# The targets of a pair on VectorE in the sparse feed-forward, and two copies in a row in the attention

## What is computed

```python
x = x + tanh(g_xattn[1]) * attention(layernorm(x), ctx)       # 16 heads of 64, 32 batches of 128 tokens
x = x + tanh(g_ffn[1]) * experts(layernorm(x))

# attention, per batch
q, k, v = inputs_q @ Wq, inputs_kv @ Wk, inputs_kv @ Wv
p = softmax(q @ k.T / 8 + rel_bias)
out = (p @ v) @ Wo

# experts: each token goes to 4 of 16 experts, and to a shared one
g, u = x @ gate_proj.T, x @ up_proj.T
y = (silu(g) * u) @ down_proj.T          # weighted, and summed over the 4 chosen
```

## Time and profile before

| | us |
|---|---|
| median of 3 runs | 1489.69 (1484.29 to 1493.74) |
| the profiled execution | 1486.57, span 1484.9 |
| attention | about 425 to 1085 us of the span |
| sparse feed-forward | about 1085 to 1485 us |

### The profile page before, as it was taken

One profiled execution on the slowest core, in us unless ns is written; L12 is line 12 of the kernel. 1 busy time (PEld: TensorE's weight loads), 2 busy tenths in 40 slices (PEclk: granted clock), 3 DMA queues, 4 the chain that ended last, 5 costly groups with the idle time before them and its releaser, 6 DMA issues. The chain is left out here.

```text
span 1484.9 us, 28060 instructions
## 1 busy us (share of the span) xinstructions
PE 1171.9 (79%) x9258; PEld 1069.9 (72%) x9258; DVE 945.7 (64%) x2039; ACT 789.5 (53%) x2201; POOL 531.4 (36%) x659
## 2 busy tenths in 40 slices
PE   3766413999489999999999998998649998778764
PEld 2555213898478888888888888897648997778664
DVE  4888594554166666656776577767757864335666
ACT  3555313555256666656665666656546675446441
POOL 4443135464200000110016510455153578788541
PEclk9676556999789999999999999999779999989896
DMA  3339772564330000010003310233176566657995
GB/s 91 114 127 259 228 132 83 144 163 132 63 98 9 9 8 1 23 30 2 8 23 125 125 30 1 75 126 123 42 249 209 162 193 192 198 167 220 293 287 208
DMA packets 139523, 177.12 MB, mean 119 GB/s; under 512 B 21984, under 2 KB 120448, under 8 KB 139392
## 3 DMA queue, kind: packets, MB, share of 16 engines
q1 hardware_dynamic: 110928, 122.62, 29.1%
q0 software_dynamic: 17792, 43.14, 9.0%
q10 hardware_dynamic: 10672, 9.65, 2.2%
HBM read 107.28 MB, written 68.09 MB: 118 GB/s over the span
## 5 line engine op out<-in xcount | busy, mean ns | idle before, releaser
L1617 ACT ACTIVATE attend_s<-attend_s,attend_less 128x128 f32<-128x128 f32 x512 | 198.4, 392 | 108.6 <-DVE attend_less L1758 108.6
L2269 POOL DMA_INDIRECT answers<-moe_yb,moe_dst x160 | 158.1, 988 | 94.2 <-ACT moe_yb L2364 56.0
L1572 POOL TENSOR_TENSOR router_xn<-rest_acc,router_mv 128x512 f32<-128x512 f32 x12 | 12.6, 1046 | 443.2 <-DVE router_rs L1234 387.1
L1635 ACT ACTIVATE attend_pt<-attend_psS 128x1024 f32<-128x1024 f32 x64 | 65.6, 1025 | 95.6 <-PE attend_psS L1909 95.4
L81 PE MATMUL moe_psU<-moe_wh,moe_xl 128*128 (+1 forms) x384 | 113.3, 295 | 0.0
L82 PE MATMUL moe_psU<-moe_wl,moe_xh 128*128 (+1 forms) x384 | 111.9, 291 | 0.0
L83 PE MATMUL moe_psU<-moe_wh,moe_xh 128*128 (+1 forms) x384 | 111.7, 291 | 0.0
L1202 POOL DMA_INDIRECT slots<-router_row,router_idx x80 | 80.6, 1007 | 79.7 <-DMA router_row<-normed_rows 61.5
L1756 DVE SCALAR_TENSOR_TENSOR attend_s<-attend_psS,held_bias 128x1024 f32<-128x1024 f32 x64 | 78.0, 1218 | 44.2 <-PE attend_psS L1902 44.1
L2422 DVE TENSOR_TENSOR moe_it<-moe_it,moe_psU 128x256 f32<-128x256 f32 x96 | 40.2, 418 | 102.8 <-ACT moe_it L2346 102.4
L81 PE MATMUL attend_psJ<-attend_xh,held_low 128*128 128x256 f32 x256 | 81.0, 316 | 26.0 <-DVE attend_q_t L1793 22.8
(11 more groups left out here) (386 smaller groups left out, 4118.5 us busy)
## 6 DMA issues: line engine op xcount, KB each, us to landing
moe_xg<-slots SPq DMA_DIRECT2D x160, 129.0 KB
moe_both<-answers SPq DMA_DIRECT2D x28, 512.0 KB, 5.1
router_row<-normed_rows SPq DMA_DIRECT2D x40, 256.0 KB, 2.9
slots<-mix_zero SPq DMA_DIRECT2D x4, 2048.0 KB, 18.4
layer_raw<-in_wi_dram SPq DMA_DIRECT2D x8, 1024.0 KB, 5.0
layer_raw<-in_wo_dram SPq DMA_DIRECT2D x8, 1024.0 KB, 7.0
moe_raw<-in_gex_dram SPq DMA_DIRECT2D x17, 384.0 KB, 4.1
moe_both<-normed_rows SPq DMA_DIRECT2D x24, 256.0 KB, 3.8
```

What stands on the lines that cost most here:

```text
L1617: last = nc.scalar.activation(s[:, g, j, :], s[:, g, j, :], ACT.Exp, bias=less[:, g, j:j + 1], accum_out=sm[:, g, j:j + 1])
L2269: nc.gpsimd.indirect_dma_start(out=R.YT[q], out_offset=bass.IndirectOffsetOnAxis(ap=dst[:, r % NM, s:s + 1], axis=0), in_=yb[:, r % NY, s, ...
```

## The change

In the attention, VectorE's second copy moves in front of normed(b, 0), so that the copies of us[0] and us[1] follow each other. In the sparse feed-forward, targets moves from GpSimd to VectorE, into turn j for pair j + 2, behind i_low(j - 1); it waits for the rows of the pair (x_in) and, from the ninth routed pair on, for the scatter of the pair 8 before (y_free). The separate wait for aside is gone, as VectorE makes that table itself. aside is laid out with the two numbers of a pair side by side.

```diff
                 evacuate(n, us[0], to(0))
+                evacuate(n, us[1], to(1))
                 normed(b, 0)
-                evacuate(n, us[1], to(1))
...
-    AHEAD = 4
...
-        aside = left[:, 2 * 3 * 64:2 * 5 * 64].bitcast(I32).rearrange("p (q s j) -> p q s j", q=2, s=2)
+        aside = left[:, 2 * 3 * 64:2 * 5 * 64].bitcast(I32).rearrange("p (q j s) -> p q j s", q=2, s=2)
...
-            for r in range(AHEAD):
-                targets(ROUTED[r])
             for r, j in enumerate(ROUTED):
-                if r + AHEAD < len(ROUTED):
-                    targets(ROUTED[r + AHEAD])
                 scatter(j)
...
+            def targets(j):
+
+                r, q = NTH[j], KIND[j]
+                dve.wait_ge(x_in[j % NX], x_count(j))
+                if r >= NM:
+                    scattered(dve, r - NM)
+                at = r - sum(TILES_OF[0:q])
+                v.tensor_tensor(dst[:, r % NM, :], xg[:, j % NX, :, D + 1].bitcast(I32), aside[:, q, at], ALU.add).then_inc(d_up, 1)
...
-                v.tensor_scalar(rows(aside[:, q]), psR[:, 3 * 64:5 * 64], lane[:], float(R.answer_rows[q]), ALU.is_gt, ALU.mult).then_inc(aside_up, 1)
+                v.tensor_scalar(aside[:, q].rearrange("p j s -> p s j"), psR[:, 3 * 64:5 * 64].rearrange("p (s j) -> p s j", s=2), lane[:], float(R.answer_rows[q]), ALU.is_gt, ALU.mult).then_inc(aside_up, 1)
...
                 if 1 <= j <= PAIRS_ALL:
                     i_low(j - 1)
+                if j + 2 < PAIRS_ALL and not is_shared(j + 2):
+                    targets(j + 2)
```

More of the change, by code:

```diff
@@ L2288, in send @@
                                              in_=row[:, h % NS, a, :], in_offset=None).then_inc(sent[h % NS], 16)
[L2290 to L2300, removed]
             nc.gpsimd.iota(steps128[:], [[P, MOST * 3]], base=0, channel_multiplier=0, **small)
```

## The result

The changed kernel took 1467.51 us (median of 4 runs, 1464.26 to 1471.58) beside 1487.12 us for the kernel before (4 runs): a ratio of 0.985 [0.982, 0.988]. Its profiled execution took 1471.58 us, with a span of 1469.9. Run again beside 17 runs of the kernel before (median 1490.88), it gave 0.9858 [0.9838, 0.9877]. So it is about 1.5% faster, clear of the noise. The chances put slightly more on "within 1%" (0.49) than on "faster" (0.46), and that was wrong.

The account below looks back on a forecast made before the run. It took TensorE, waiting for VectorE's copies, to bound the attention, and TensorE, GpSimd, SyncE, then DMA the sparse feed-forward. Attention -14.7 and feed-forward -1.8 made -16.5 us: 1486.57 to 1470, plus 3.1 for the median, 1473; range 1465 to 1484.

Parts of the forecast that it names:

- The other five have one long wait in place of two ...: nothing: Attention, five router-middle half-steps where VectorE comes late from router work (one wait 2.66 us): no gain.
- the four of the table's last row: Attention half-steps 0, 19, 29 and 30, the remaining ones: about 1 us less in all.
- 0.71 and 0.83 us a half-step: Attention without router middle: gain when TensorE's second wait goes, 0.71 us for q, 0.83 for k, counted between starts.
- rival 2: Attention: TensorE gains only its idle entries, 9 us, because something held for slack (o_low) binds; 1479 us, chance 0.14.
- ScalarE's hold on the router middles: Attention: with router rows in the middle, the output product awaits ScalarE's last copy, leaving 0.26 of 0.71 us.
- Half-steps with the router's inverse, near 0.9: Attention: three k half-steps with the router's inverse between the copies would gain near 0.9 us each.
- rival 3: Attention: fewer stops let TensorE keep its clock, 6.8 us more gained in four half-steps; 1466 us, chance 0.08.
- The sparse feed-forward, -1.8 us: Moving targets: -3.2 us in the send stretch, +1.2 in the first stretch, +0.2 behind the last answers.
- The 1.2 us of loss in the first stretch: Sparse feed-forward, 1139 to 1205 us: about 23 new VectorE adds, half of them felt, cost 1.2 us.
- Rival 1: Sparse feed-forward: each new VectorE add blocks a GpSimd DMA issue 0.15 us, 4.8 us in all; 1478 us, chance 0.14.
- rule against the change: Sparse feed-forward: VectorE instructions with two SBUF inputs block GpSimd's SBUF reads; a DMA issue took 1.41 us, not 0.98.
- The wait for y_free, nothing: Sparse feed-forward: VectorE's wait for an earlier pair's scatter costs nothing; a loop of about 7 us against 24 for 6 pairs.

Follow-up runs that it names:

- e1: The kernel before with only the attention's new copy order: 1470.17 us, ratio 0.9873 to the kernel before.
- e2: The changed kernel with the old copy order put back, so only the sparse feed-forward is changed: 1487.42 us, ratio 0.9975 to the kernel before.
- e7: The changed kernel with ScalarE's last copy ahead of its last four exponentials in half-steps with router middles: 1463.84 us, ratio 0.983 to the kernel before.
- e6_twice: The kernel before with GpSimd's add of targets made twice, the first into a buffer nobody reads: 1493.89 us, ratio 1.0025.
- e3_again: The changed kernel run once more, unaltered, on the same chip as its two parts: 1470.66 us, ratio 0.9858 to the kernel before.
- e4_sixteen: The changed kernel with 16 buffers for the targets in place of 8: 1470.29 us, ratio 0.9862 to the kernel before.
- e11_scalar: A repeat of the changed kernel with ScalarE's last copy ahead of its last four exponentials in router middles: 1466.99 us, ratio 0.9819 to the kernel before.
- e5_four: The changed kernel with 4 buffers for the targets in place of 8: 1582.31 us, ratio 1.0608 to the kernel before.
- e8_late: The changed kernel with both VectorE copies between the two biased products in half-steps 16, 22, 24, 28 and 29: 1475.15 us, ratio 0.9897 to the kernel before.

## Why the prediction was right or wrong

**The step that failed.** It is a term of the count that was put at nothing: "The other five have one long wait in place of two ...: nothing". These five half-steps took 3.9 us less, and the four of the table's last row 3.3 where about 1 was given: together 6.2 us too little. In their place the runs show what one profile could not. VectorE's product was held by GpSimd's in some executions and not in others, and with the new order no copy stood behind it any more. TensorE's clock fell less often. And two half-steps had a second wait that could go. Against these 6.2 us, the rows of the router's inverse and of the router middles were priced 2.3 us too high, so that errors of opposite sign helped the time to fall into the range: some of that is luck. The attention was forecast at 14.7 us and measured at 18.0 by the traces and 18.9 by the times.

**What bounds the kernel.** Right. Both parts moved what they were said to move, in the places named (e1, e2).

**0.71 and 0.83 us a half-step.** Right for q: the five without a router middle took 0.71 us less each. For k, 0.78 in place of 0.83. The idle entries alone (0.46 and 0.49) would have been too little, which rules rival 2 out: counting from start to start is what gave the right size. ScalarE's hold on the router middles was right too (e7).

ScalarE's hold took more than was allowed for it, though: the nine half-steps gave 1.9 us and not about 3. Half-step 28 gave nothing (20.42 before, 20.50 after), where its second wait of 0.45 us went and one of 0.48 for ScalarE came in (the changed kernel's profile).

**Half-steps with the router's inverse, near 0.9.** Wrong: 0.48. The prediction looked for what is late next among the waits, and here a collision was next. GpSimd's normalising for the router starts when VectorE has its inverse ready. In the kernel before, VectorE's product (L1763) started ahead of GpSimd's second product, and GpSimd was held: the timelines of VectorE and GpSimd, half-step 9,

```profile
609.84 1.46 DVE L1763 TENSOR_TENSOR attend_s<-attend_s,attend_rc 128x1024 f32<-128x1024 f32 x1
...
609.18 1.04 POOL L1572 TENSOR_TENSOR router_xn<-rest_acc,router_mv 128x512 f32<-128x512 f32 x1 [207.56 <-DVE router_rs L1234]
610.30 1.90 POOL L1574 TENSOR_TENSOR router_xn<-router_xn,router_rs 128x512 f32<-128x512 f32 x1
```

With the two copies in a row VectorE's product comes 0.04 us behind GpSimd's, and VectorE is held:

```profile
605.67 2.08 DVE L1763 TENSOR_TENSOR attend_s<-attend_s,attend_rc 128x1024 f32<-128x1024 f32 x1
...
605.63 1.04 POOL L1574 TENSOR_TENSOR router_xn<-router_xn,router_rs 128x512 f32<-128x512 f32 x1
```

2.08 us in place of 1.22; o_low behind it is late, and TensorE waits for attend_ol before the output product. At the transposes ahead of that product the half-step is 0.96 us in front of the kernel before (10.04 us into it, not 11.00), so the 0.9 held that far; at the product only 0.47 is left (11.32, not 11.79). The idle entry there is 0.20 us, which again understates it. The Trainium skill (SBUF — State Buffer, Who interferes with whom) says that VectorE and GpSimd share a pair of ports, and that whoever issues first has it for the whole instruction while the other one blocks. These two meetings agree with it, GpSimd's first product counted in (VectorE's 1.46 us began while that one ran). The collisions further down do not. The prediction knew of this contention, but weighed it only for the new adds.

**"The other five have one long wait: nothing."** Two things stand in these half-steps that the prediction, from one profile, held for fixed.

The first is again the collision. In half-steps 18 and 19 GpSimd's normalising stands behind its indirect DMAs, and its start moves from execution to execution (7.2 us into half-step 18 in the kernel before, 6.7 in the changed one, 8.3 in e2_feed). In the old order VectorE's product stood between the two copies. When it was hit, the second copy was late, and TensorE with it: e2_feed (VectorE, then GpSimd),

```profile
796.50 2.83 DVE L1763 TENSOR_TENSOR attend_s<-attend_s,attend_rc 128x1024 f32<-128x1024 f32 x1
799.24 0.68 DVE L1793 COPY attend_q_t<-attend_psJ 128x512 f32<-128x512 f32 x1
...
797.18 1.05 POOL L1572 TENSOR_TENSOR router_xn<-rest_acc,router_mv 128x512 f32<-128x512 f32 x1
798.31 1.91 POOL L1574 TENSOR_TENSOR router_xn<-router_xn,router_rs 128x512 f32<-128x512 f32 x1
```

That half-step took 24.66 us, and half-step 19 of e6_twice 25.65 in the same way (a product of 2.79 us). In the new order the product is hit just as well (2.19 us in half-step 19 of e3_again, 2.38 in e4_sixteen), but the copies are through, and those half-steps took 20.69 and 20.77. Half-steps 18 and 19 together took 45.2 us on average in the old order and 41.1 in the new one: 4.1 of the 18.0 us. In both of the old order's long ones the late copy made a stop of 2.1 us, and TensorE's clock fell behind it: from that stop on, half-step 18 of e2_feed took 3.2 us longer than that of e6_twice from its own (1.04 us), and half-step 19 of e6_twice 3.1 longer than that of e2_feed from the same place. Over three executions that is 2.1 us: by this estimate about half of the 4.1 us is the clock, and the rest the late copy. No run took the collision away by itself; this is read from the durations.

In this pair of lines VectorE's product began 0.68 us ahead of GpSimd's first one and was held all the same, while GpSimd's took its usual 1.05 us. The order of the recorded starts does not say who is held here. What does hold in every such meeting is the end: of VectorE's products (L1763; 1.22 us undisturbed), 66 took over 1.3 us in the attention of the thirteen executions, and each of them ended 1.08 to 1.10 us behind the end of a GpSimd product, whichever of the two had begun first.

The second is TensorE's clock by itself, rival 3. Half-step 16 has the same stop in both kernels, 2.66 and 2.65 us. Before, the matmuls behind it were slow; in the changed kernel they are not. A window behind the stop, of the kernel before and then of the changed one (columns as in the earlier trace rows):

```profile
752.30:758.00 5.70, 5.70 (x37) 5.60 (x37) 3.75 (x7) 5.11 (x20) 0.00 (x0) 0.74 0.00 0
```

```profile
744.70:749.90 5.20, 4.66 (x37) 4.32 (x37) 3.69 (x8) 5.20 (x23) 0.00 (x0) 1.00 0.00 0
```

Timeline of TensorE, the changed kernel:

```profile
744.80 0.39 PE L81 MATMUL attend_psJ<-attend_xh,held_low 128*128 128x256 f32 x1 [2.65 <-DVE attend_q_t L1793]
745.26 0.29 PE L81 MATMUL attend_psJ<-attend_xh,held_low 128*128 128x256 f32 x1
745.62 0.28 PE L81 MATMUL attend_psJ<-attend_xh,held_low 128*128 128x256 f32 x1
```

and e11_scalar, where they are slow again:

```profile
744.64 0.58 PE L81 MATMUL attend_psJ<-attend_xh,held_low 128*128 128x256 f32 x1 [2.65 <-DVE attend_q_t L1798]
745.45 0.42 PE L81 MATMUL attend_psJ<-attend_xh,held_low 128*128 128x256 f32 x1
746.09 0.41 PE L81 MATMUL attend_psJ<-attend_xh,held_low 128*128 128x256 f32 x1
```

Three matmuls are 0.36 us apart in the one and 0.64 in the other. The third projection, 12 matmuls, takes 2.73 us and not 1.53 (1.2 more, not the 1.7 of the prediction, whose 3.23 us spanned 15 matmuls), and the half-step 0.6 us more, since a stop of 0.44 us for ScalarE comes back where the matmuls are fast. The granted clock behind the stop is 1.00 in the changed kernel and 0.74 in the kernel before, a mean over the higher level (2.4 GHz) and the lower (1.2 GHz). In half-step 16 it fell in 3 of 3 executions with the old order, in 1 of 6 with the new one (e5_four, 1.4 us behind the stop), and in 3 of 3 with ScalarE's copy moved as well.

Over the 31 half-steps the clock stood at the lower level for 27.3 to 30.7 us in the three executions of the old order and for 10.2 to 20.5 in the six of the new one. What a fall cost is read from the same half-step with and without it, and it is weighed by how often it came. This estimate gives the new order 0.5 us in half-step 16, 0.3 in 22, 0.2 in 24 and about 1 in 30 (granted clock 0.78 to 0.79 over that half-step in the old order, 0.88 and 0.89 in the changed kernel's two profiles), and takes 0.5 from it in 29. That is about 1.5 us, and with the 2 of half-steps 18 and 19 about 3.6 of the 18.0. So rival 3 was right in kind, and its 6.8 us were about twice too much. What decides whether the clock falls after a stop of the same length, no run here shows.

Not all was collision or clock. In half-steps 26 and 29 the executions at the higher level took 0.8 us less with the new order (21.22 against 20.10 to 20.60, and 20.86 against 20.09, a mean). Both have a second wait of 0.5 to 0.6 us in the old order, and in 26 the profile that the prediction was made from shows only the first.

**The sparse feed-forward, -1.8 us.** The 3.2 us of the send stretch were right (3.4), and e6 confirms the price from the other side. The 1.2 us of loss in the first stretch were wrong: 80 adds of 155 ns found room on VectorE even where it is busy 0.8 of the time. The part measured 3.7 us (from 1.0 to 6.6 by its interval). From the scores of half-step 31 to the end, the traces of the old targets give 430.6 and 429.2 us (the kernel before, e1), eight with the new ones 424.4 to 432.8, on average 428.2: 1.7 us less, within their scatter. So the term is right in sign and in size as far as can be told.

Rival 1, the adds hold up GpSimd, falls: an indirect DMA of answers took 982 ns on average in the changed kernel and 988 before. Seven began while one of the new adds was running, and took 0.96 to 0.97 us each; none of the 47 issues of sends or answers in which an add began took over 0.99. The long issues, such as the 1.41 us of the earlier trace rows, are still there (up to 1.48), beside VectorE's sums in combine. So the prediction's rule against the change held for those and not for the new adds.

**The wait for y_free, nothing.** The result was right, and the argument's number wrong: the loop is about 17 us when nothing holds it and 19 to 23 with four buffers, not 7, because the pair's whole way from VectorE's add to GpSimd's scatter belongs to it. The prediction counted only the work between the landing and the next answers. Its sign of being wrong, VectorE standing before the add, came true at 69.9 us and cost nothing (e4). An idle entry of an engine that does not limit was no sign at all. Another of its signs meant something: o_low took over part of the gain in the half-steps with the router's inverse.

**The base and the chances.** The sum gave 16.5 us; 19.6 came out in the first comparison and 21.2 in the second. The line of 1% lies 14.9 us below the kernel before, so the whole verdict hung on whether the forecast, 1.6 us beyond it (the prediction has 1.5), was too low or too high. What was put at nothing (long stops, collisions, the clock) could mostly make the gain larger, and it had 0.08 in all. With 6.2 us left out on that side and 2.3 us too much on the other, "within 1%" was the wrong side to favour.

## What to carry to other kernels

When an engine's order is changed, list what else ran at the times that its instructions leave and enter, not only who waits for them: here a product that was slowed in both orders stopped TensorE only while a copy stood behind it (24.66 and 25.65 us for a half-step, against 20.69 and 20.77). Before a buffer's wait is called free, follow the buffer once around, from its filling to its release, and compare with the pace: a turn of about 17 us fits into 8 buffers at 3.2 us a pair; 4 cost 111 us, and the turn itself was then 19 to 23 us. And take the base from several profiles where half-steps of the same code differ by microseconds: one profile gave 15.7 us for what was 18.0.

## What the runs showed of the hardware

- A VectorE instruction of 128x8 with a single input tensor was held as well: L1758, otherwise 0.17 us, took 1.72 at 791.56 in the kernel before and 1.28 at 783.00 in the changed one. Both ended with GpSimd's first normalising product (792.18 + 1.06 and 783.20 + 1.05), though they had begun 0.62 us ahead of it in the one and 0.20 in the other.
- Of the 66 slowed products of VectorE above, 10 had begun ahead of the GpSimd product that they ended behind, by up to 0.68 us (796.50 in e2_feed).
- Between two indirect DMAs of GpSimd lie 0.30 us. An add of 0.20 us put into that gap makes it 0.40: half of it is hidden there, and only of the first one.
- A stop of TensorE of 2.65 to 2.67 us in half-step 16 was followed by the higher clock in five executions and by the lower one in seven (e8_late, where the stop lies elsewhere, is the thirteenth).
